# Attention values turned by DMA instead of TensorE, and weight splitting moved to GpSimd, in a fused two-layer transformer kernel

## The chip, the cores and the metric

The kernel runs on one core of a Trainium2 chip. The metric is the device time of one execution in microseconds (us), as the median of several runs. One execution computes all 16 sequences.

## What is computed

The input is `x`, 16 sequences of 256 tokens with 512 features, with a condition vector per sequence. Two blocks follow each other. Cut to what matters:

```python
# block 0
h = layernorm(x) * (1 + scale) + shift
q = h @ Wq.T                      # 16 heads of 32
c = h @ Wkd.T; k = c @ Wku.T; v = c @ Wvu.T   # 4 key/value heads
q, k = rope(q), rope(k)
y = softmax(masked(q @ k.T / sqrt(32))) @ v   # window of 64, block-causal, every 64th key
x = x + y @ Wo.T
# block 1
h = rms(x) * gain1
q, k, v = h @ Wq1.T, h @ Wk1.T, h @ Wv1.T     # 8 heads of 64, one key/value head
x = x + softmax(rope(q) @ rope(k).T / 8) @ v @ Wo1.T
h = rms(x) * gain2
x = x + (silu(h @ Wg.T) * (h @ Wu.T)) @ Wd.T  # inner width 2048
```

"Weighted values", or heads, are `y`: the attention output of all heads of a tile of 128 tokens, a 128x512 matrix, just before the product with `Wo` or `Wo1`.

## The kernel before, in words

**Arithmetic.** Every fp32 operand of a product is split into a high and a low fp16 half, and `product` (L1384 to L1386) issues three matmuls: high by high, high by low, low by high. A product wants its left operand with the features on the partitions, so activations that lie with tokens on the partitions are turned first. Splitting costs one ScalarE copy (the high half) and one VectorE subtraction (the low half).

**Rounds.** Sequences are worked in 8 pairs. A round does both attention blocks of a pair, and among their steps, piece by piece, the MLP of the pair before. The MLP has 96 parts (`mlp_part`, L1594) of 6 matmuls each: 64 for the gate and up products (four parts for each of 16 chunks) and 32 for the down product. `PLAN` (L124) says by hand how many parts go with each named step; `between(m, step)` issues them ahead of that step's own work, on TensorE (L1643) and the matching gate, tanh and sum operations on VectorE and ScalarE. The first round has no MLP to mix in, and after the eighth round the last MLP runs alone.

**Attention.** Each block is a row of units, 24 in block 0 and 16 in block 1. Unit j goes through: scores on TensorE (L1448 or L1454) into one of four PSUM banks; minimum on VectorE; exponentials on ScalarE (L853); high half on ScalarE (L862) and low half on VectorE (L1083) into one of three slots of `prob`; a DMA transpose issued by SyncE (L574, `turn_probs`); values on TensorE into `ybank`. Scores run two units ahead, values four behind. The four banks and the three slots are handed out in a fixed order (`ORDER`, and the unit's number modulo 3), and each use waits until the use before it in the same place is over.

**Heads.** When the values of a tile (s, t) of sequence s and token tile t are complete, `normalise` (VectorE, L1123) writes them to `work`. Then TensorE turns them with four fp32 transposes into the next PSUM bank (`heads`, L1415, shown as L1419), ScalarE takes the high half (`heads`, L839, shown as L842), VectorE the low half (`heads_low`, L1057, shown as L1061), and `project` (L1519) multiplies by `Wo`. For t = 0 this happens inside the unit loop at the units of `FILL_AT` (20 and 22 in block 0, 12 and 14 in block 1); for t = 1 in `finish` (L1504), which is the end of each block: last values, `out{layer}a` projections of t = 0, heads of t = 1, `out{layer}b` projections of t = 1. After these come residual add (L1141), squares on ScalarE (L996), the root on GpSimd (L691), scaling (L1260) and the transposes of the next stage, `fill`.

**Weights.** In the first round weights are loaded by SyncE as fp32 into staging areas and split: most in 128x512 pieces by ScalarE and VectorE (`PIECES_AT`, L151: eight pieces for `wq1` and `wo1`, shown as L1003 and L1335), the four 1 MB groups `wd0` to `wd3` by GpSimd (`big_split_`, L754; per group four operations each at L758, L761 and L766). `SPLIT_AT`, `LOADS_AT` and `RAW_AT` (L156 to L174) name the step at which GpSimd splits, and SyncE loads, a group or one of the first two raw chunks of the gate and up weights. In the second round GpSimd splits these chunks (L734 to L751) as they are first used.

SyncE issues every DMA, in the order of `PLAN`, from one queue.

Of the kernel before, what the change touches and what calls it, by code (L numbers as in the profile page):

```python
# [14 lines left out]
P = 128  # L15
# [46 lines left out]
FILL_AT = [{20: 0, 22: 1}, {12: 0, 14: 1}]  # L62


def unit_uses(layer):
    uses = [(f"unit{layer}", j) for j in range(AHEAD)]
    for j in range(UNITS[layer]):
        if j + AHEAD < UNITS[layer]:
            uses.append((f"unit{layer}", j + AHEAD))
        if j in FILL_AT[layer]:  # L70
            uses.append((f"heads{layer}", FILL_AT[layer][j], 0))
    return uses
# [5 lines left out]
         + unit_uses(0) + [("out0", s, 0) for s in BOTH] + [("heads0", s, 1) for s in BOTH]  # L78
         + [("out0", s, 1) for s in BOTH]
         + [("fill2", s, b) for s in BOTH for b in range(2)] + [("kv1", s) for s in BOTH]  # L80
         + unit_uses(1) + [("out1", s, 0) for s in BOTH] + [("heads1", s, 1) for s in BOTH]
         + [("out1", s, 1) for s in BOTH] + [("fill4", s, b) for s in BOTH for b in range(2)])
# [4 lines left out]
HI_ORDER = ([("fill0", s, b) for s in BOTH for b in range(2)]  # L87
            + [name for layer in range(2) for name in (
                [use for j in range(UNITS[layer]) for use in (
                    [(f"unit{layer}", j)] + [(f"heads{layer}", FILL_AT[layer][k], 0)  # L90
                                             for k in FILL_AT[layer] if k == j])]
                + [(f"heads{layer}", s, 1) for s in BOTH]
                + [(f"fill{2 + 2 * layer}", s, b) for s in BOTH for b in range(2)])])
HI_USE = {name: m for m, name in enumerate(HI_ORDER)}
HI_USES = len(HI_ORDER)
LOW_ORDER = [name for name in HI_ORDER if name[0][:4] != "unit"]
# [8 lines left out]
def last_read(name):  # L105

    kind, k = name[0], name[1]
    if kind[:4] == "unit":
        return "prob_split", sum(UNITS), unit_index(int(kind[4]), k) + 1
# [4 lines left out]
    if kind in ("kv", "kv1"):  # L114
# [9 lines left out]
PLAN = [("fill0.0", 0), ("fill0.1", 3), ("lat.0", 3), ("lat.1", 2), ("kv.0", 2), ("kv.1", 1),  # L124
# [1619 lines left out]
```

## Time and profile before

| | before |
|---|---|
| median of 3 runs | 1868.71 us (1867.02 to 1870.58) |
| the profiled execution's own time | 1865.45 us |
| its span | 1863.6 us |
| TensorE (PE) busy | 1730.3 us, 93% |
| VectorE (DVE) busy | 1148.2 us, 62% |
| ScalarE (ACT) busy | 941.9 us, 51% |
| GpSimd (POOL) busy | 375.1 us, 20% |
| DMA queue of SyncE, share of 16 engines | 57.1% |

The rounds follow from where the transposes of `fill4` (L1411) stand: the first round ends at about 214 us, the second at 442 us, the following six take 211 to 218 us each, and the last MLP runs from 1736 us on. Reported times of neighbouring matmuls overlap, because their ends are modelled; what a matmul costs is the distance from its start to the next one's start. PEclk is the granted TensorE clock, 1.00 being 2.4 GHz and 0.50 being 1.2 GHz.

### The profile page before, as it was taken

What the parts mean: (1) busy time and instruction counts of PE and PEld (TensorE: products, weight loads), DVE (VectorE), ACT (ScalarE), POOL (GpSimd) and SP (SyncE); (2) the same over time, 40 slices, a digit from 0 to 9 for tenths busy, and PEclk for the clock granted to TensorE, in tenths of its full rate; (3) what the DMA queues carried; (4) which work ended last, traced back from release to release, by engine and by line L of the source; (5) the groups of instructions that cost most, each with busy time, mean ns of one, the idle gap of its engine ahead of it and who ended that gap; (6) DMA issues with size and microseconds to landing.
All of it is one profiled execution on the core that took longest, in us unless ns stands there. A gap on an engine that the chain in (4) does not pass through costs nothing.

```text
span 1863.6 us, 38242 instructions
## 1 busy us (share of the span) xinstructions
PE 1730.3 (93%) x12496; PEld 956.0 (51%) x12496; DVE 1148.2 (62%) x2960; ACT 941.9 (51%) x2783; POOL 375.1 (20%) x530
## 2 busy tenths in 40 slices
PE   6675998999999999999999999999999999999999
PEld 5543544455455544555455654555445554555444
DVE  5668567575676647675576746776476745757320
ACT  3646447354574547554483545645374544826320
POOL 2343377111110111110110111111111111101120
PEclk9577999999999999999999999999999999999999
DMA  5965479461793538663584717844386625936220
GB/s 180 218 157 100 132 178 228 123 121 55 161 181 90 82 99 187 144 107 83 120 184 92 120 68 156 173 97 79 107 190 132 113 74 133 185 89 108 96 69 23
DMA packets 527352, 234.51 MB, mean 126 GB/s; under 512 B 476432, under 2 KB 493840, under 8 KB 527120
## 3 DMA queue, kind: packets, MB, share of 16 engines
q1 hardware_dynamic: 527120, 231.72, 57.1%
q8 instruction: 108, 1.77, 0.4%
q14 instruction: 124, 1.02, 0.2%
HBM read 90.09 MB, written 16.78 MB: 57 GB/s over the span
## 4 chain that ended last, share of the span: by engine, by line
PE 70%; DMA 10%; DVE 7%; ACT 5%; issue 4%; SPq 3%; POOL 0%; DVEq 0%; ACTq 0%
PE up L1384 7%; PE gate L1386 7%; PE gate L1384 7%; PE gate L1385 7%; PE up L1385 7%; PE up L1386 7%; DMA prob_t<-prob 7%; PE y L1384 4%; PE y L1386 4%; PE y L1385 4%; PE bank L1384 3%; PE bank L1386 3%; PE bank L1385 3%; PE bank L1411 2%; ACT bank L853 2%
## 5 line engine op out<-in xcount | busy, mean ns | idle before, releaser
L853 ACT ACTIVATE bank<-bank,low 128x128 f32<-128x128 f32 (+2 forms) x768 | 303.9, 397 | 85.2 <-DVE low L1076 71.5
L697 POOL TENSOR_TENSOR inner_t<-inner,inner_t 128x512 f16<-128x512 f32 x128 | 148.5, 1160 | 697.0 <-ACT inner_t L1021 697.0
L1083 DVE TENSOR_TENSOR prob<-bank,prob 128x512 f16<-128x512 f32 (+1 forms) x320 | 203.1, 635 | 71.5 <-ACT prob L862 69.2
L862 ACT ACTIVATE prob<-bank 128x512 f16<-128x512 f32 (+1 forms) x320 | 179.1, 560 | 89.6 <-DMA prob_t<-prob 63.2
L1384 PE MATMUL up<-mlp,ring 128*128 128x512 f16 x512 | 195.3, 381 | 10.6 <-DVE inner L1351 10.6
L1341 DVE SCALAR_TENSOR_TENSOR silu<-silu,gate 128x512 f32<-128x512 f32 x128 | 87.9, 687 | 181.6 <-ACT silu L1015 181.6
L1384 PE MATMUL gate<-mlp,ring 128*128 128x512 f16 x512 | 195.0, 381 | 0.8 <-POOL ring L751 0.7
L1386 PE MATMUL gate<-mlp,ring 128*128 128x512 f16 x512 | 195.5, 382 | 0.0
L1385 PE MATMUL gate<-mlp,ring 128*128 128x512 f16 x512 | 195.4, 382 | 0.0
L1385 PE MATMUL up<-mlp,ring 128*128 128x512 f16 x512 | 194.9, 381 | 0.0
L1386 PE MATMUL up<-mlp,ring 128*128 128x512 f16 x512 | 194.7, 380 | 0.0
L853 ACT ACTIVATION_READ_ACCUMULATOR bank<-bank,low 128x1 f32 x768 | 159.8, 208 | 0.0
L1072 DVE CUSTOM_DVE_ANT_0 bank<-bank,mask 128x193 f32<-128x193 f32 (+1 forms) x512 | 152.3, 351 | 5.8 <-PE bank L1448 5.8
L1015 ACT ACTIVATE silu<-gate 128x512 f32<-128x512 f32 x128 | 76.0, 594 | 136.1 <-PE gate L1386 129.6
L1351 DVE SCALAR_TENSOR_TENSOR inner<-up,silu 128x512 f32<-128x512 f32 x128 | 88.1, 688 | 85.5 <-PE up L1386 78.2
L996 ACT ACTIVATE work<-x_mid 128x512 f32<-128x512 f32 x64 | 40.3, 630 | 177.0 <-DVE x_mid L1141 177.0
L1384 PE MATMUL y<-v_hi,prob_t 128*128 128x32 f16 (+2 forms) x1024 | 110.6, 186 | 18.3 <-DMA prob_t<-prob 13.0
L1021 ACT ACTIVATE inner_t<-inner 128x512 f16<-128x512 f32 x128 | 81.2, 634 | 77.9 <-DVE inner L1351 77.9
L1385 PE MATMUL y<-v_lo,prob_t 128*128 128x32 f16 (+2 forms) x1024 | 109.2, 185 | 0.0
L1386 PE MATMUL y<-v_hi,prob_t 128*128 128x32 f16 (+2 forms) x1024 | 109.1, 185 | 0.0
L1076 DVE TENSOR_REDUCE low<-bank 128x2 f32<-128x512 f32 x128 | 86.9, 684 | 32.8 <-PE bank L1454 32.7
L1384 PEld LDWEIGHTS y<-v_hi,prob_t 128*128 128x128 f16 (+1 forms) x1024 | 91.4, 99 | 29.6 <-DMA prob_t<-prob 19.2
(166 smaller groups left out, 4039.0 us busy)
## 6 DMA issues: line engine op xcount, KB each, us to landing
ring<-wgu_dram SPq DMA_DIRECT2D x112, 512.0 KB, 3.7
x_in<-x_dram SPq DMA_DIRECT2D x18, 512.0 KB, 5.8
x_res<-x_mid SPq DMA_DIRECT2D x16, 512.0 KB, 3.0
wgu_dram<-ring SPq DMA_DIRECT2D x16, 512.0 KB, 3.6
out_dram<-x_res SPq DMA_DIRECT2D x32, 256.0 KB, 3.0
prob_t<-prob SPq DMA_TRANSPOSE x256, 3.3
inner_t<-wd_t_dram SPq DMA_DIRECT2D x8, 512.0 KB, 4.7
ring<-wg_t_dram SPq DMA_DIRECT2D x16, 256.0 KB, 3.8
```

Of the source, the lines that this page charges most:

```text
L697: pool.tensor_tensor(inner_t[:, 1, f, :], inner[:], inner_t[:, 0, f, :], ALU.subtract).then_inc(inner_low, 1)
L853: ins = act.activation(bank_[:, at:at + wid], bank_[:, at:at + wid], ACT.Exp, bias=low[:, j % BANKS, k:k + 1], scale=-1.0, accum_out=total)
L862: act.activation(terms(prob[:, g % SLOTS, 0, :], layer, j), terms(work_bank[USE[f"unit{layer}", j] % BANKS][:], layer, j), ACT.Copy).then_ ...
L1021: act.activation(inner_t[:, 0, f, :], inner[:], ACT.Copy).then_inc(inner_high, 1)
L1072: ins = dve.tensor_tensor_reduce(out=view, in0=view, in1=mask[:, 0:wid], scale=1.0, scalar=3.0e38, op0=ALU.add, op1=ALU.min, accum_out=low ...
L1076: ins = dve.tensor_reduce(low[:, j % BANKS, 0:2], bank_[:].rearrange("p (h k) -> p h k", h=2), AX.X, ALU.min)
L1083: dve.tensor_tensor(terms(prob[:, slot, 1, :], layer, j), terms(work_bank[USE[name] % BANKS][:], layer, j), terms(prob[:, slot, 0, :], lay ...
L1341: dve.scalar_tensor_tensor(silu[:], silu[:], 1.0, gbank[:], ALU.add, ALU.mult).then_inc(gated, 1)
L1351: dve.scalar_tensor_tensor(inner[:], ubank[:], 0.5 * HS / (WS * WS), silu[:], ALU.mult, ALU.mult).then_inc(inner_ready, 1)
L1384: pe.matmul(out_ap, left[0], right[0], start=start, stop=False)
L1385: pe.matmul(out_ap, left[0], right[1], start=False, stop=False)
L1386: return pe.matmul(out_ap, left[1], right[0], start=False, stop=stop)
```

## The change

The TensorE transposes of the heads are gone. ScalarE now takes the high half of `work` in token order into a slot of `prob`, VectorE the low half beside it, and SyncE issues one DMA transpose of both halves (eight blocks of 128x128 fp16) into the operand `act` of the projection. The heads no longer take one of the four PSUM banks, but do take one of the three `prob` slots, so that units and heads together are numbered (`SPLIT`). In block 0 the heads of t = 0 move from units 20 and 22 to 13 and 15.

`wq1` and `wo1` are split by GpSimd, at the start of the first round, in place of ScalarE and VectorE. Loads and splits of the `wd` groups and of the first two raw chunks move from the units of block 0 to its end and beyond. `PLAN` is dealt out anew. The diff, cut to its core (of `PLAN` the end of block 0 and of block 1 are shown whole; among the rest, units 12 to 16 of block 0 go from 1, 1, 1, 1, 2 parts to 2, 3, 1, 2, 0, and `query3.1`, `stack2.0`, `scores1`, units 2, 5 and 11 of block 1 lose one part each):

```diff
-FILL_AT = [{20: 0, 22: 1}, {12: 0, 14: 1}]
+HEADS_AT = [{13: 0, 15: 1}, {12: 0, 14: 1}]
...
-        if j in FILL_AT[layer]:
-            uses.append((f"heads{layer}", FILL_AT[layer][j], 0))
...
+SPLIT_ORDER = split_order(0) + split_order(1)
+SPLIT = {name: m for m, name in enumerate(SPLIT_ORDER)}
+SPLITS = len(SPLIT_ORDER)
...
-        ("out0a.0", 0), ("out0a.1", 0), ("heads0.0", 1), ("heads0.1", 0), ("out0b.0", 0),
-        ("out0b.1", 0), ("fill2.0", 2), ("fill2.1", 1), ("kv1.0", 1), ("kv1.1", 0),
+        ("out0a.0", 0), ("out0a.1", 0), ("heads0.0", 1), ("heads0.1", 0), ("out0b.0", 2),
+        ("out0b.1", 0), ("fill2.0", 2), ("fill2.1", 0), ("kv1.0", 1), ("kv1.1", 0),
...
-        ("unit1_14", 1), ("unit1_15", 0), ("out1a.0", 0), ("out1a.1", 0), ("heads1.0", 2),
-        ("heads1.1", 0), ("out1b.0", 1), ("out1b.1", 0), ("fill4.0", 2), ("fill4.1", 1)]
+        ("unit1_14", 1), ("unit1_15", 0), ("out1a.0", 0), ("out1a.1", 1), ("heads1.0", 3),
+        ("heads1.1", 1), ("out1b.0", 0), ("out1b.1", 0), ("fill4.0", 1), ("fill4.1", 1)]
...
-             "unit0_1": range(10, 11),
-             "out0a.0": range(11, 13), "out0a.1": range(13, 15), "unit1_1": range(15, 16),
-             "unit1_3": range(16, 17), "unit1_5": range(17, 18), "unit1_7": range(18, 19)}
-BIG = [f"wd{c}" for c in range(CH)]
-SPLIT_AT = {"fill2.0": BIG}
+             "unit0_1": range(10, 11)}
+BIG = ["wq1", "wo1"] + [f"wd{c}" for c in range(CH)]
+SPLIT_AT = {"fill0.0": BIG[:2], "heads0.0": BIG[2:3], "kv1.0": BIG[3:5], "unit1_6": BIG[5:]}
...
-LOADS_AT = {"keys.1": [("wkv1", 0), ("wkv1", 1)], "unit0_1": [("wd0", 0)],
-            "unit0_2": [("wd0", 1)], "unit0_4": [("wd1", 0)], "unit0_5": [("wd1", 1)],
-            "unit0_7": [("wq1", 0)], "unit0_8": [("wq1", 1)], "unit0_10": [("wd2", 0)],
-            "unit0_11": [("wd2", 1)], "unit0_14": [("wd3", 0)], "unit0_15": [("wd3", 1)],
-            "fill2.0": [("wo1", 0), ("wo1", 1)]}
-RAW_AT = {"unit0_18": 0, "unit0_20": 1}
+LOADS_AT = {"lat.0": ["wkv1"], "kv.0": ["wo1"], "out0a.0": ["wd0"], "out0a.1": ["wd1"],
+            "heads0.0": ["wd2"], "heads0.1": ["wd3"]}
+RAW_AT = {"fill2.0": 0, "kv1.0": 1}
...
-            for key in ("tw1", "tw2", "wo0"):
+            for key in ("wo0", "tw1", "tw2", "wq1"):
...
+            def turn_heads(n, layer, s, t):
+                split = SPLIT[f"heads{layer}", s, t]
+                need_apart(sp, prob_split, count(n, SPLITS, split + 1), (cond_used, 1))
+                sp.dma_start(act_both[s][:, :, :, t * P:(t + 1) * P].rearrange(
+                    "p a c q -> p (a c) q"), prob[:, split % SLOTS].rearrange("p a k -> p (a k)"),
+                             transpose=True).then_inc(heads_in[s], 16)
...
             def heads(n, layer, s, t):
-                use = USE[f"heads{layer}", s, t]
-                need(act, full, count(n, USES, use + 1))
-                act.activation(act_t[s][0][:, :, t * P:(t + 1) * P],
-                               work_bank[use % BANKS][:].rearrange("p (c q) -> p c q", c=CH),
+                name = (f"heads{layer}", s, t)
+                need(act, weighted, count(n, 8, 4 * layer + 2 * t + s + 1))
+                turned_before(act, n, name)
+                act.activation(prob[:, SPLIT[name] % SLOTS, 0, :], work[:, s, t, :],
                                ACT.Copy).then_inc(hi_done, 1)
...
             def heads_low(n, layer, s, t):
...
-                dve.tensor_tensor(act_t[s][1][:, :, cols],
-                                  work_bank[use % BANKS][:].rearrange("p (c q) -> p c q", c=CH),
-                                  act_t[s][0][:, :, cols], ALU.subtract).then_inc(low_made, 1)
+                dve.tensor_tensor(prob[:, slot, 1, :], work[:, s, t, :], prob[:, slot, 0, :],
+                                  ALU.subtract).then_inc(prob_split, 1)
...
-            def heads(n, layer, s, t):
-                bank_ = bank_for(n, f"heads{layer}", s, t)
-                need(pe, weighted, count(n, 8, 4 * layer + 2 * t + s + 1))
-                for c in range(CH):
-                    ins = pe.transpose(bank_[:, c * P:(c + 1) * P],
-                                       work[:, s, t, c * P:(c + 1) * P], ident[:])
-                ins.then_inc(full, 1)
...
             def project(n, layer, s, t, w):
                 bank_ = bank_for(n, f"out{layer}", s, t)
-                need(pe, low_made, count(n, LOW_USES, LOW_USE[f"heads{layer}", s, t] + 1))
+                need(pe, heads_in[s], heads_count(n, layer, t))
                 token_major(bank_[:], act_t[s], t, w, D).then_inc(full, 1)
```

## Rows read from the trace of the kernel before

Columns of a busy-time row: the stretch, its length, busy us and instructions of PE, PEld (weight loads), DVE, ACT and POOL, then PEclk, DMA share, GB/s. Columns of a timeline row: start, us, engine, line, operation, what it writes and reads, how many.

**Rows 1.** Busy time by stretch: first round, a middle round, the last MLP alone.
```profile
0.00:214.00 214.00, 143.96 (x1127) 101.36 (x1128) 141.02 (x380) 114.02 (x341) 73.61 (x120) 0.77 0.69 162
...
869.00:1087.00 218.00, 210.11 (x1546) 114.48 (x1546) 139.24 (x364) 115.74 (x345) 30.75 (x45) 0.99 0.58 121
...
1736.00:1864.00 128.00, 124.36 (x577) 56.15 (x574) 25.54 (x37) 21.34 (x35) 18.50 (x16) 1.00 0.20 68
```

**Rows 2.** Waits, 442 to 1736 us (six rounds): us in total, times, longest.
```profile
ACT prob L862 <- DMA prob_t<-prob: 38.1, 39, 2.7
...
PE bank L1448 <- DVE prob L1083: 7.0, 12, 1.2
...
PE bank L1384 <- DVE act_lo L1061: 4.8, 6, 1.0
...
PE bank L1419 <- DVE prob L1083: 3.5, 3, 1.5
```

**Rows 3.** TensorE's timeline around eight of the heads' transposes.
```profile
1070.96 1.04 PE L1419 MATMUL bank<-ident,work 128*128 128x128 f32 x8
1071.84 0.38 PE L1384 MATMUL up<-wd_hi,inner_t 128*128 128x512 f16 x1
```

**Rows 4.** Timeline at the end of block 0 and of block 1, a middle round.
```profile
990.88 0.38 PE L1384 MATMUL gate<-mlp,ring 128*128 128x512 f16 x1
...
991.46 0.24 DVE L1127 RECIPROCAL inv<-sums 128x16 f32<-128x16 f32 x1
...
1068.37 0.38 PE L1384 MATMUL up<-wd_hi,inner_t 128*128 128x512 f16 x1
...
1069.09 0.69 DVE L1129 TENSOR_TENSOR work<-y,inv 128x512 f32<-128x512 f32 x1
```

**Rows 5.** Line L574, the DMA transposes of `prob`: durations of the issue, time to landing.
```profile
L574 SPq DMA_TRANSPOSE prob_t<-prob x256: 1231/1237/3755, 61.2 to 1710.5; - x128
...
DMA to landing us min/median/max: 3.0/3.3/6.4
```

**Rows 6.** Busy time by stretch at the ends of the two blocks.
```profile
990.00:994.00 4.00, 2.90 (x37) 1.89 (x33) 2.91 (x6) 1.81 (x4) 0.00 (x0) 1.00 0.00 0
1068.00:1072.00 4.00, 3.99 (x33) 2.53 (x34) 1.71 (x5) 1.12 (x3) 0.00 (x0) 1.00 0.00 0
```

**Rows 7.** SyncE's timeline in the first round, units of block 0.
```profile
82.44 2.09 SPq L574 DMA_TRANSPOSE x_mid<-prob  x1
...
110.16 4.11 SPq L574 DMA_TRANSPOSE prob_t<-prob  x3
```

**Rows 8.** DMA issues by line, 84 to 110 us: KB, us to landing.
```profile
prob_t<-prob SPq DMA_TRANSPOSE x9, 4.8
```

**Rows 9.** DMA queues and issues, 154 to 196 us, units of block 1.
```profile
q1 hardware_dynamic: 16896, 4.20, 58.6%
...
prob_t<-prob SPq DMA_TRANSPOSE x12, 3.2
```

**Rows 10.** Busy time by stretch, two pieces of the first round.
```profile
8.00:10.00 2.00, 1.07 (x6) 1.10 (x6) 0.00 (x0) 0.00 (x0) 1.75 (x4) 1.00 1.04 403
32.00:34.00 2.00, 1.63 (x10) 1.29 (x11) 0.77 (x4) 0.13 (x1) 0.00 (x0) 0.50 0.00 0
```

**Rows 11.** The chain that ended last, first round, end of block 0.
```profile
119.12 0.70 DVE work L1129
...
121.25 0.70 DVE act_lo L1061
...
122.09 0.38 PE bank L1384
```

**Rows 12.** Groups by line: VectorE's pieces of the `wo` weights.
```profile
L1335 DVE SCALAR_TENSOR_TENSOR wo_lo<-inner_t,wo_hi 128x512 f16<-128x512 f32 x8 | 5.3, 694 | 3.9 <-ACT wo_hi L1003 3.9
```

**Rows 13.** Line L766, GpSimd's low halves of `wd`: ns min, median, max.
```profile
L766 POOL TENSOR_TENSOR wd_lo<-inner_t,wd_hi x16: 1150/1152/1154, 77.0 to 111.5; 128x512 f16<-128x512 f32 x16
```

**Rows 14.** Line L1171, VectorE's sums of two fp32 operands in SBUF.
```profile
L1171 DVE TENSOR_TENSOR work<-work x96: 281/681/1639, 39.6 to 1671.6; 128x512 f32<-128x512 f32 x64, 128x256 f32<-128x256 f32 x16, 128x128 f32<-128x128 f32 x16
```

More of the change, by code:

```diff
@@ L256, in build @@
         work = sb("work", [P, PAIR, TILES, D])
-        act_t = [halves(f"act{s}", [P, CH, TOK]) for s in BOTH]
+        act_both = [sb(f"act{s}", [P, 2, CH, TOK], F16) for s in BOTH]
+        act_t = [(a[:, 0], a[:, 1]) for a in act_both]
         mlp = sb("mlp", [P, 2, CH, PTOK], F16)
@@ L397, in build @@
                "wkv1": (0, [(wide(wk1_t), CH, HD1, 0), (wide(wv1_t), CH, HD1, CH * HD1)]),
-               "wq1": (0, by_two(wq1_t)), "wo1": (0, by_two(wo1_t))}
-        for k, key in enumerate(BIG):
-            at = int(key[-1])
-            raw[key] = ((3, 1, 2, 3)[k], by_two(wd_t[at * D:(at + 1) * D, :]))
+               "wq1": (3, [(wide(wq1_t), CH, D, 0)]), "wo1": (1, [(wide(wo1_t), CH, D, 0)])}
+        for c, slot in enumerate((2, 3, 1, 0)):
+            raw[f"wd{c}"] = (slot, [(wide(wd_t[c * D:(c + 1) * D, :]), CH, D, 0)])
         landed, older, got = {}, {}, (STAGES + 2) * [0]
@@ L409, in build @@
             (key, w, p * PIECE, p * PIECE, PIECE) for key, w, pieces in (
-                ("wq0", wq0, 4), ("wo0", wo0, 4), ("wkv1", None, 1), ("wq1", wq1, 4),
-                ("wo1", wo1, 4)) for p in range(pieces)]
+                ("wq0", wq0, 4), ("wo0", wo0, 4), ("wkv1", None, 1)) for p in range(pieces)]
         def staged(key):
@@ L437, in big_views @@
         def big_views(key, half):
-            slot, at = staged(key), int(key[-1])
-            return [(slot[:, c * D:(c + 1) * D],
-                     flat(wd[half])[:, (at * CH + c) * D:(at * CH + c + 1) * D])
+            slot = staged(key)
+            w, at = ((wq1, 0) if key == "wq1" else (wo1, 0) if key == "wo1" else
+                     (wd, int(key[-1]) * CH))
+            return [(slot[:, c * D:(c + 1) * D], flat(w[half])[:, (at + c) * D:(at + c + 1) * D])
                     for c in range(CH)]
@@ L480, in _, with load @@
         def _(sp):
-            def load(key, which=None):
+            def load(key):
                 slot, parts = raw[key]
@@ L484, in load @@
                     split_wait(sp, k)
-                for src, chunks, cols, at in parts if which is None else [parts[which]]:
+                for src, chunks, cols, at in parts:
                     dst = staged(key)[:, at:at + chunks * cols]
@@ L569, in turn_probs @@
                 g = unit_index(layer, j)
-                need_apart(sp, prob_split, count(n, sum(UNITS), g + 1), (cond_used, 1))
+                split = SPLIT[f"unit{layer}", j]
+                need_apart(sp, prob_split, count(n, SPLITS, split + 1), (cond_used, 1))
                 need_apart(sp, pv_done, count(n, sum(UNITS), g - TURNED + 1), (cond_used, 1))
@@ L647, in _ @@
                 turn((None, 0), step)
-                for key, which in LOADS_AT.get(step, ()):
-                    load(key, which)
+                for key in LOADS_AT.get(step, ()):
+                    load(key)
                 if step in RAW_AT:
@@ L1080, in prob_lows @@
             def prob_lows(n, layer, j):
[L1081 removed]
+                name = (f"unit{layer}", j)
+                slot = SPLIT[name] % SLOTS
                 need(dve, hi_done, count(n, HI_USES, HI_USE[name] + 1))
```

83 lines of the change are left out of this document (46 added, 37 removed), and 20 rows, old and new, of the table PLAN.

## The prediction, made before the changed kernel was run

> **What bounds the kernel now.** I read busy time by stretch first [rows 1]. In a middle round TensorE is busy 210 of 218 us, so whatever leaves its queue is gained there, as long as no wait takes its place. The first round is another matter: 144 of 214 us, a mean clock of 0.77 and DMA engines at 0.69; it is set by chains of waits. The last MLP, 96 parts in 128 us, gives the price of one part, 1.33 us; I take 1.3. It isn't touched. Next come the waits of the six middle rounds [rows 2]: TensorE waits little, but four kinds of wait there belong to what the change moves. Last I read the timeline at the ends of the blocks, since that is where the heads of t = 1 stand between the last values and the next projection with nothing but MLP parts to cover them [rows 4].
>
> **Middle rounds: what is removed.** Eight transposes take the distance from 1070.96 to 1071.84, 0.88 us [rows 3]. A round has 8 heads of 4, that is 32, so 3.5 us of TensorE's queue go.
>
> Three waits go too [rows 2], each divided by six rounds. The projection's wait for `act_lo`, 4.8 us, is 0.8 per round. The transposes' wait for a PSUM bank (DVE prob L1083), 3.5 us, is 0.6. The scores' wait for a bank, 7.0 us, is 1.2; where heads take a bank, the scores behind them get one that was released a unit later, and without heads this shift is gone. Not all of it stems from there, so I take 0.7 (bounds 0 and 1.2). Together 2.1.
>
> **Middle rounds: what is added.** The heads of t = 0 are asked for several units after they are ready and cost TensorE nothing; that rests on SyncE and the slots keeping pace (a rival below). For t = 1 the new path is: both normalisations, the high half on ScalarE beside the second of them, the low half, SyncE's issue, the transpose, the projection. What is queued behind the projection's wait is all of TensorE's work. Behind SyncE's wait for the low half are only loads and stores with rounds of slack; the issue itself holds SyncE 1.24 us [rows 5], eight times a round.
>
> In block 0 the second reciprocal starts at 991.46 and lasts 0.24; with 0.69 for the normalisation it ends at 992.42 [rows 4]. A low half of 0.70 [rows 11] and 0.1 for SyncE (estimate) give 993.2. From issue to landing takes 3.0 at best, 3.3 in the median and 6.4 at worst [rows 5]. I take 3.3, because in exactly these stretches the DMA engines are idle, share 0.00 [rows 6]; so 996.5. TensorE is through with the values at 990.88 and has three parts, 3.9 us, until 994.8. New wait: 1.7 us (1.4 at the best landing, 4.8 at the worst).
>
> In block 1 the second normalisation ends at 1069.78; the same steps give 1073.9. TensorE has four parts from 1068.37 on, until 1073.6. New wait: 0.3 (0 to 3.4). The second sequence's heads are issued 1.24 later and are covered by the first projection, which is as long as two parts (24 issues; 2.6 us).
>
> The parts dealt out anew uncover other places: `fill2.1` and `fill4.0` lose one part each, just where the scaled residual is awaited. One part is 1.3, so the bounds are 0 and 2.6 together; I take 0.6. Block 1 starts its units three parts earlier, with VectorE idle until then, but sends two more uses through three slots; 0.4, bounds -1 and 3.
>
> Sum for a round: -3.5 - 2.1 + 1.7 + 0.3 + 0.6 + 0.4 = **-2.6**. Seven rounds carry an MLP: **-18.2**. The second round has more on the DMA engines, but gets the same.
>
> **First round.** Its MLP-free chain gains and loses.
>
> Units of block 0. SyncE turns unit 9 at 82.44, and units 21 to 23 from 110.16 to 114.27, the last from about 113 on [rows 7]: 2.2 us a unit. In this stretch a transpose lands after 4.8 us [rows 8]; in block 1, without loads between, after 3.2 [rows 9]. There the queue was used for 58.6% of 42 us by 16 transposes: 1.54 us each, a limit even without loads. Once the loads are moved away I expect 1.65 a slot, but the two heads (units 13 and 15) take slots too: 16 x 1.65 = 26.4 in place of 14 x 2.2 = 30.6, so -4.2 (bounds -8 and 0, the latter if ScalarE sets the pace).
>
> End of block 0. From the end of the first normalisation, 119.82, to the projection at 122.09 took 2.3 us [rows 11]. Now: second normalisation 0.93, low half 0.70, 0.1, landing 3.3, together 5.0: +2.7. Two groups `wd0` and `wd1` are loaded ahead of it; at 403 GB/s [rows 10] a megabyte takes 2.7 us, so they are through about when the heads are issued. `wd2` stands in SyncE's queue between the two heads: the second lands 1.24 + 0.6 + 2.7 = 4.5 after the first, of which the first projection covers 2.6: +1.9. Together +4.6 (bounds 2.5 and 10). End of block 1: +2.7, with nothing loaded there.
>
> Splitting of `wq1` and `wo1`. Eight pieces of 0.69 leave VectorE [rows 12] and eight copies ScalarE. The four of `wq1` lay beside a projection and give nothing; the four of `wo1` lay in the units of block 1. 4 x 0.69 = 2.8 at most; I take -1.5.
>
> GpSimd instead. Its low halves last 1.15 each [rows 13]. VectorE's sums of two operands that both lie in SBUF have a median of 0.68 but a longest of 1.64 [rows 14]: they are held up by up to 1 us. Before, GpSimd split the `wd` groups during the units of block 0, where VectorE reads PSUM. Now it splits `wq1` and `wo1` during the first queries and keys, and `wd1` and `wd2` during those of block 1, where such sums and subtractions stand on the chain, some 12 in each place. At 0.2 us each that is +5 (bounds 0 and 15). The Trainium skill has a rule for this (SBUF — State Buffer, SBUF: two separate sides): VectorE and GpSimd share a port pair under an exclusive lock that is held for a whole instruction, and VectorE needs it when it has two SBUF inputs while GpSimd reads SBUF. The spread in that row agrees with it.
>
> Clock. The clock was at 0.50 in 32:34, after TensorE had been short of work [rows 10]. The two new waits of 5 us may bring the same, with projections at half speed for a while: +1.5 (0 to 5).
>
> Sum: -4.2 + 4.6 + 2.7 - 1.5 + 5 + 1.5 = **+8.1**.
>
> **Forecast.** -18.2 + 8.1 = -10.1. The profiled execution took 1865.45, so 1855.4; the median of the runs lies 3.3 above it, so **1858.6** as a median.
>
> **Rivals.**
>
> Much more gained. All four waits go entirely (-2.6), and the new ones are covered by parts as dealt: -5.2 a round with 0.9 of new waits, -36 in seven rounds, first round even: 1833. For it: the DMA engines are idle at the places that matter, and VectorE is idle before block 1's units. Against it: the sum above leaves block 0 uncovered by 1.7.
>
> Slower, at the ends of the blocks. The place is the projection of t = 1, 14 times in seven rounds. If the transpose lands after 4.8, as under load, and not 3.3, each costs 1.5 more: +21, so 1880. It decides from 10.1 / 14 = 0.7 more on, a landing of 4.0. Against it: share 0.00 [rows 6]; for it: the destination is cut into more places than before, and `act` was never written by a DMA. The Trainium skill speaks against the change itself (VectorE: DVE Perf Modes, Rules for kernel authors): a 128x128 transpose belongs on TensorE if PSUM will do as destination, and on the DMA only otherwise. Read by duration that would make this rival the likely one; the rows above make it depend on cover.
>
> Slots. ScalarE already waits for a slot 38.1 us in six rounds [rows 2], and none of it reaches TensorE. Four more uses at 1.5 us are 6 us a round. Should half of this reach TensorE: +21, again 1880.
>
> First round worse. Splits and subtractions hold each other up at their bound, +10 more, 1869; or GpSimd comes late to the root: 1874.
>
> The change doesn't do what it says. If the round is really paced by ScalarE and VectorE and TensorE merely looks full, the 3.5 us turn into waits: about +8 in all, 1877. TensorE's few waits speak against it.
>
> **How the numbers follow.** The forecast with its neighbours (1850 to 1867) gets 0.42, much more gained 0.20, the end of the blocks 0.14, the slots 0.05, the first round 0.12, no effect 0.07. A measurement of this kernel can tell about 0.2%, 3.7 us. Faster by more than that, below 1865.0: the forecast nearly whole, and the second case, 0.62. Within it: part of the first-round case and the edge of the forecast, 0.13. Slower, above 1872.4: 0.25. The range leaves out a tenth at either end: 1838 to 1878.
>
> **What would show it.** Right: no L1419 in the profile; TensorE's waits for the DMA into `act` near 1.7 us at the end of block 0 and under 1 at the end of block 1; middle rounds of 213 to 214 us by the distance of their `fill4` transposes; a first round of about 222 us, with the units of block 0 shorter by 4 us and VectorE's L1171 and L1238 longer there. Wrong: a landing above 4 us in the middle rounds, waits of ScalarE for slots that TensorE's scores inherit, or a first round that is not longer.

## The result: slower, and outside the range

The median of the changed kernel is 1883.43 us (1879.21 to 1885.25, four runs) against 1869.3 of the kernel before (1867.02 to 1870.58): ratio 1.007, 95% interval 1.0051 to 1.0089. Forecast were 1858.6 us and a range of 1838 to 1878.

The page of the kernel after. A group of section 5 reads: line, engine, operation, tiles, count | busy us, mean ns of one | idle just before them and what ended most of it.

```profile
PE 1712.4 (91%) x12240; PEld 924.2 (49%) x12240; DVE 1150.1 (61%) x2952; ACT 941.8 (50%) x2775; POOL 401.8 (21%) x554
...
q1 hardware_dynamic: 594608, 248.51, 61.0%
...
L1405 PE MATMUL bank<-wo_hi,act 128*128 128x512 f16 x256 | 100.7, 393 | 35.8 <-DMA act<-prob 35.3
...
L1461 PE MATMUL bank<-k_t,q_t 96*128 96x193 f16 (+1 forms) x512 | 71.8, 245 | 42.9 <-DVE prob L1104 30.1
```

The heads' transposes are gone, and before the projection (L1405) TensorE now sits idle for 35.3 us until the DMA into `act` has landed; only the scores (L1461) have a longer idle time. L1405 is the line of the first product (before: L1384), L1461 the scores, L883 and L1104 ScalarE's and VectorE's split of the probabilities, L863 and L1082 that of the heads.

The waits of the six middle rounds, 450 to 1750 us of the kernel after (us, times, longest), beside [rows 2]:

```profile
PE bank L1405 <- DMA act<-prob: 18.7, 21, 1.9
PE bank L1461 <- DVE prob L1104: 13.4, 16, 1.4
PE bank L1432 <- issue: 7.9, 5, 1.8
...
PE gate L1405 <- DVE silu L1362: 5.2, 6, 1.1
PE y L1405 <- DMA prob_t<-prob: 4.7, 11, 0.9
...
PE y L1405 <- DMA x_mid<-prob: 2.7, 3, 1.2
...
ACT prob L883 <- DMA prob_t<-prob: 70.8, 59, 2.5
...
ACT prob L883 <- DMA x_mid<-prob: 31.6, 18, 3.5
```

ScalarE's waits for a slot of `prob` went from 38.1 (46.6 with those ended by the turns into `x_mid`) to 102.4. The scores' wait rose from 7.0 to 13.4. The heads' own path, as bounded in [rows 5], is on the page of its line:

```profile
L592 SPq DMA_TRANSPOSE act<-prob x64: 1231/1246/1990, 89.9 to 1735.3; - x64
...
DMA to landing us min/median/max: 3.1/3.2/6.5
```

Where the time lies is best seen by rounds: the distance from the first transpose of `stack` by TensorE to the first of the next round. "First" goes from the start of the span to the second round's mark, "middle" is the mean of five rounds, "rest" goes from the last such mark to the end of the span. These are us of one profiled execution; the last column is the median of the runs.

| kernel | heads | slots | first | second | middle | rest | median |
|---|---|---|---|---|---|---|---|
| before | TensorE | 3 | 207.8 | 229.6 | 216.1 | 345.5 | 1869.3 |
| after | DMA | 3 | 218.0 | 224.9 | 218.4 | 342.6 | 1883.4 |
| plan_only | TensorE | 3 | 207.4 | 224.8 | 215.5 | 342.4 | 1849.3 |
| weights_only | TensorE | 3 | 202.5 | 229.1 | 217.8 | 345.0 | 1868.1 |
| plan_and_weights | TensorE | 3 | 203.1 | 223.5 | 215.1 | 341.6 | 1845.4 |
| heads_and_plan | DMA | 3 | 224.4 | 226.8 | 218.9 | 343.7 | 1894.1 |
| tensor_slots4 | TensorE | 4 | 199.8 | 220.4 | 212.4 | 339.2 | 1824.8 |
| slots4 | DMA | 4 | 217.1 | 222.9 | 215.3 | 338.8 | 1860.2 |
| t0_by_dma | t=0 DMA | 3 | 211.8 | 228.0 | 216.8 | 343.6 | 1870.3 |
| t1_by_dma | t=1 DMA | 3 | 212.9 | 225.8 | 215.5 | 343.1 | 1862.8 |

So the first round grew by 10.2 us from before to after, the middle rounds by 2.3 each; the second round and the rest became shorter by 4.7 and 2.9.

### The profile page after: what moved, and what is told of

It reads as the page before. It is cut to its first block, busy times and chain, and to the rows that moved or that the text cites. A ratio compares the mean times of both kernels' runs of the same rounds, so it can differ in the third digit from the quotient of the medians.

```text
span 1877.4 us, 37983 instructions
## 1 busy us (share of the span) xinstructions
PE 1712.4 (91%) x12240; PEld 924.2 (49%) x12240; DVE 1150.1 (61%) x2952; ACT 941.8 (50%) x2775; POOL 401.8 (21%) x554
## 4 chain that ended last, share of the span: by engine, by line
PE 55%; DMA 16%; DVE 11%; issue 7%; ACT 6%; SPq 4%; DVEq 0%; POOL 0%; ACTq 0%
DMA prob_t<-prob 8%; PE gate L1405 5%; PE gate L1407 5%; PE gate L1406 5%; PE up L1405 5%; PE up L1406 5%; PE up L1407 5%; DMA act<-prob 5%; PE bank L1405 4%; PE bank L1407 3%; PE bank L1406 3%; PE y L1405 3%; PE y L1407 3%; PE y L1406 3%; SPq L585 3%
## 5 line engine op out<-in xcount | busy, mean ns | idle before, releaser
L1104 DVE TENSOR_TENSOR prob<-bank,prob 128x512 f16<-128x512 f32 (+1 forms) x320 | 203.2, 635 | 104.3 <-ACT prob L883 103.3
L883 ACT ACTIVATE prob<-bank 128x512 f16<-128x512 f32 (+1 forms) x320 | 178.4, 558 | 143.7 <-DMA prob_t<-prob 91.3
L1405 PE MATMUL gate<-mlp,ring 128*128 128x512 f16 x512 | 195.1, 381 | 6.1 <-DVE silu L1362 5.2
L1405 PE MATMUL up<-mlp,ring 128*128 128x512 f16 x512 | 195.8, 382 | 5.3 <-DVE inner L1372 5.3
L1372 DVE SCALAR_TENSOR_TENSOR inner<-up,silu 128x512 f32<-128x512 f32 x128 | 88.0, 688 | 86.8 <-PE up L1407 79.0
L1405 PE MATMUL bank<-wo_hi,act 128*128 128x512 f16 x256 | 100.7, 393 | 35.8 <-DMA act<-prob 35.3
L1405 PE MATMUL y<-v_hi,prob_t 128*128 128x32 f16 (+2 forms) x1024 | 110.3, 186 | 15.3 <-DMA prob_t<-prob 13.2
L1461 PE MATMUL bank<-k_t,q_t 96*128 96x193 f16 (+1 forms) x512 | 71.8, 245 | 42.9 <-DVE prob L1104 30.1
```

Source lines behind the costliest of these rows:

```text
L883: act.activation(terms(prob[:, SPLIT[name] % SLOTS, 0, :], layer, j), terms(work_bank[USE[f"unit{layer}", j] % BANKS][:], layer, j), ACT.C ...
L1104: dve.tensor_tensor(terms(prob[:, slot, 1, :], layer, j), terms(work_bank[USE[name] % BANKS][:], layer, j), terms(prob[:, slot, 0, :], lay ...
L1372: dve.scalar_tensor_tensor(inner[:], ubank[:], 0.5 * HS / (WS * WS), silu[:], ALU.mult, ALU.mult).then_inc(inner_ready, 1)
L1405: pe.matmul(out_ap, left[0], right[0], start=start, stop=False)
```

## The experiments

**Which part of the change did it.** Four kernels hold the new heads (H), the new table of parts `PLAN` (P) and the new splitting and loading of the weights (W) in different mixtures. weights_only is before with W, plan_only before with P, heads_only before with H, heads_and_plan after without W.

```diff
 # weights_only: of the change only this, with the loads that go with it
-SPLIT_AT = {"fill2.0": BIG}
+SPLIT_AT = {"fill0.0": BIG[:2], "heads0.0": BIG[2:3], "kv1.0": BIG[3:5], "unit1_6": BIG[5:]}
 # plan_only: of the change only the numbers of PLAN, as
-("unit1_2", 1), ("unit1_5", 2), ("unit1_11", 1), ("unit1_12", 1)
+("unit1_2", 0), ("unit1_5", 1), ("unit1_11", 0), ("unit1_12", 2)
```

> The kernel before with the weights part of the change alone: wq1 and wo1 split by GpSimd, wd and raw chunks loaded later; heads stay on TensorE, PLAN as before. Theory (shared SBUF port): the first round grows by 5 to 8 us because VectorE's two-operand sums during the first queries and keys are held up; median 1874 to 1877; the sum L1171/L1192 reaches 1.5 us or more before 60 us. Rival (the first round's extra 10 us come from the heads): no change, 1869 within 2. The middle rounds stay at 216 us under both.

> Only PLAN dealt out as in the change; heads on TensorE, weights as before. Theory: fewer parts in block 1 leave its units to ScalarE's pace, so middle rounds grow by 0 to 3 us, median 1869 to 1890. Rival (the new PLAN is better in itself, and the loss is all in the DMA path): below 1869.

> The changed kernel with the weights part undone (wq1, wo1 by ScalarE and VectorE, wd split early). Theory: the first round falls by 5 to 8 us against the changed kernel, middle rounds keep their 218 us; median 1875 to 1878. Rival: as slow as the changed kernel, 1883.

> Only the heads turned by DMA; weights and PLAN as before. At the end of block 0 one part covers the new path instead of three, at the end of block 1 two instead of four: theory (uncovered path) says 2.6 us more of waiting in each, less what the parts give elsewhere; middle rounds of 219 to 222 us, median 1885 to 1900. Rival (slots of prob set the pace, cover does not matter): like heads_and_plan, within 4 us of it.

Measured: weights_only 1868.12, ratio 0.9996 (0.9974 to 1.0019); plan_only 1849.25, 0.9902 (0.9865 to 0.994); heads_and_plan 1894.08, 1.0146 (1.0108 to 1.0184); heads_only 1979.46, 1.0609 (1.0568 to 1.065). Of the four theories only the sign of the heads' cost held. weights_only took the time of its rival (no change), plan_only fell where its rival had it (below 1869), heads_and_plan lies above both of its cases, and heads_only is 79 us above the top of its theory. The table of parts, which I had taken for a detail, brings about 1%; the heads cost more than all else. heads_only shows how tightly the two are bound: with the old table the projections wait 9.3 us a round for `act` (3.1 in after), and the middle rounds last 230 us.

**The best without the heads.** plan_and_weights is after with the heads on TensorE again.

```diff
-                need(pe, heads_in[s], heads_count(n, layer, t))
+                need(pe, low_made, count(n, LOW_USES, LOW_USE[f"heads{layer}", s, t] + 1))
 # and heads(...) with its four pe.transpose of work into a bank, at the old places,
 # in block 0 units 20 and 22; so H below is the DMA together with the move to units 13 and 15
```

> The kernel after with the heads (weighted values) turned on TensorE as before: the new plan and the new splitting of the first round's weights stay. If the change's three parts add, the turn of the heads by DMA alone costs what separates this kernel from the kernel after: plan alone gave 0.990 of before, and the weights part took 5.3 us off the first round when it stood alone and 6.4 us off it beside DMA heads. Expected: first round ended at 202 +- 2 us, and 1838 to 1846 us in all, 0.983 to 0.988 of before. The rival, from weights_only, where the whole time stayed the same though the first round was 5.3 us shorter: what the weights part gains in the first round is given back later, and this kernel stands at 1847 to 1852 us.

Measured: 1845.44 (1840.98 to 1846.22), ratio 0.9873 (0.9846 to 0.99), the first round 203.1. So in the final mixture P gives -18 (against before in its own series, 1867.5), W -4 and H +38, together +16 where the result shows +14. W is the weak one of the three: -4 here, -11 beside DMA heads, 0 alone, and only its gain in the first round (4 to 6 us) shows in all three pairs of profiles.

The waits of plan_and_weights, 450 to 1740 us:

```profile
PE bank L1439 <- DVE prob L1074: 9.2, 7, 1.6
...
PE bank L1402 <- issue: 2.2, 5, 0.6
...
PE y L1375 <- DMA prob_t<-prob: 0.9, 2, 0.6
```

These are the scores, the fill's transposes and the values: 1.5, 0.4 and 0.2 us a round, against 2.2, 1.3 and 0.8 in after; and in after 3.1 us for `act`, 0.9 for `silu` and 0.5 for `x_mid` come on top. Only 1.3 us a round of waits for banks and low halves before the heads' transposes and the projections go. The busy time by stretch (450 to 1740) says the same in one number, TensorE's idle time:

```profile
450.00:1740.00 1290.00, 1257.20 (x9252) 682.33 (x9250) 826.22 (x2160) 693.45 (x2054) 187.67 (x269) 0.99 0.59 124
```
```profile
450.00:1740.00 1290.00, 1222.50 (x8993) 652.34 (x8992) 824.33 (x2163) 685.43 (x2046) 182.36 (x263) 1.00 0.63 132
```

The first fence is plan_and_weights, 32.8 us idle in 6.00 rounds; the second is the kernel after, 67.5 in 5.91. That is 5.5 and 11.4 us a round: 5.9 us of new idle time for 3.5 us of transposes. By the table the round is 3.3 us longer.

**Slots, or the tiles?** The rise of ScalarE's waits pointed to the slots. slots4 is after with a fourth one, laid on the latent buffers; t0_by_dma and t1_by_dma are after with only one tile's heads by DMA. In t1_by_dma the first tile's heads, back on TensorE, stay in block 0 at units 13 and 15, where after turns them by DMA; in plan_and_weights they stand at 20 and 22. So its distance from plan_and_weights holds this move too.

```diff
 # slots4
-        SLOTS, TURNED = 3, LAG + 1
-        prob = sb("prob", [P, SLOTS, 2, 512], F16)
+        SLOTS, TURNED = 4, LAG + 1
+        prob = sb("prob", [P, SLOTS - 1, 2, 512], F16)   # the fourth slot lies in lat_all
 # t0_by_dma (t1_by_dma: (1,)); the other tile's heads on TensorE, HEADS_AT as in after
+DMA_T = (0,)
```

> The kernel after with four slots for the split probabilities and values in place of three (the fourth lies on the latent buffers, which are free while the units run). Theory 'slots': heads share the three slots with the units, each slot is held until SyncE's turn has landed (3 to 6.5 us), and ScalarE waits for slots 102 us over the middle rounds against 47 before; then most of the 2.2 us of a middle round that separate the kernel after from plan_only come back, the middle round falls from 218.4 to 216.5 or less, the first round from 218.0 to under 212, and the kernel takes 1850 to 1866 us. Rival 'latency at the block ends': the wait is for the turn of the last heads itself, with nothing left to do beside it, and a fourth slot doesn't shorten that: ScalarE's waits for slots fall under 50 us and the time stays within 1876 to 1886 us.

> The kernel after with only the heads of the first tile of a block (t=0, which come due while units still run) by DMA; those of the second tile (t=1, at the end of the block) on TensorE again, 16 transposes of them in place of 32. Theory 'block ends': the exposed part is the second tile's turn, about 3 us in a middle round and 10 us in the first; without it 1850 to 1862 us, faster than before, first round ended at 204 to 210. Theory 'slots and SyncE's queue': half of the cost stays, 1862 to 1874 us.

> The reverse: only the heads of the second tile by DMA, those of the first tile on TensorE. Theory 'block ends': all of the cost stays and the gain of 16 transposes goes: 1880 to 1890 us, first round ended at 216 to 222. Theory 'slots and SyncE's queue': half the uses of slots go, and it comes to 1862 to 1874 us.

Measured: slots4 1860.22 (ratio 0.9952, 0.9934 to 0.997), t0_by_dma 1870.31 (1.0017, 1.0 to 1.0034), t1_by_dma 1862.8 (0.9971, 0.9955 to 0.9986). The number for slots4 is the one that the theory of the slots gave, and ScalarE's waits for slots in it fell from 102 to 23 us. t1_by_dma, for which the theory of the block ends wanted 1880 or more, fell where the slots wanted it. On these three alone I would have called the slots the cause. The control says otherwise:

```diff
 # tensor_slots4: the same edit of the slots in plan_and_weights
-                             prob[:, g % SLOTS].rearrange("p a k -> p (a k)"),
+                             prob_slots[g % SLOTS].rearrange("p a k -> p (a k)"),
```

> The control for the fourth slot: plan_and_weights (heads on TensorE, new plan, new splitting) with four slots for the probabilities in place of three. ScalarE waits 47 us for slots over the middle rounds there. Theory 'three slots are short only because of the heads': the fourth slot gives at most 0.5 us a round here against 3.3 us a round with the heads in the slots, so 1841 to 1846 us, and heads by DMA with four slots (1860.2 us) remain 14 to 19 us slower than heads on TensorE. Rival 'three slots are short in either kernel': 1825 to 1838 us.

Measured: 1824.82 (1823.26 to 1825.7), ratio 0.9769 (0.9745 to 0.9792). The rival holds. The fourth slot is worth 21 us with heads on TensorE and 23 with heads by DMA; the heads cost 38 us with three slots and 35 with four. Slots are short in either kernel; they are at most a small part of why the heads by DMA are dear. tensor_slots4 also beats both kernels of this case.

The waits of tensor_slots4, and then of slots4, 450 to 1740 us:

```profile
PE bank L1443 <- DVE prob L1078: 4.4, 6, 1.0
...
PE bank L1406 <- issue: 2.7, 5, 0.6
```
```profile
PE bank L1409 <- DMA act<-prob: 19.1, 18, 2.1
PE bank L1436 <- issue: 7.8, 5, 1.9
...
PE y L1409 <- DMA x_mid<-prob: 4.8, 6, 1.3
...
PE y L1409 <- DMA prob_t<-prob: 3.1, 8, 1.0
...
PE y L1409 <- DMA x_mid<-lat_all: 1.1, 3, 0.5
```

With slots in plenty the wait for `act` alone is 19.1 us in six rounds, 3.2 a round: nearly the 3.5 us that the transposes cost.

**The two tiles with four slots, and the place.** t0_slots4 and t1_slots4 join both edits. t0_late has three slots and moves the first tile's heads of block 0.

```diff
 # t0_late, on t0_by_dma
-HEADS_AT = [{13: 0, 15: 1}, {12: 0, 14: 1}]
+HEADS_AT = [{17: 0, 19: 1}, {12: 0, 14: 1}]
```

> t0_by_dma with four slots: only the first tile's heads by DMA. With three slots they cost 24.9 us against heads on TensorE (1870.3 against 1845.4). Theory 'the first tile hurts by holding slots': with four they cost at most 8 us, 1825 to 1833 us, and nearly all of slots4's 35 us is the second tile's bare latency. Rival 'SyncE's order and latency hurt, not the slots': 1840 to 1852 us.

> t1_by_dma with four slots: only the second tile's heads by DMA. With three they cost 17.4 us (1862.8 against 1845.4). Theory 'bare latency at the ends of the blocks, whatever the slots': 15 to 28 us more than tensor_slots4, 1840 to 1853 us, with the first round 9 us or more longer than its 199.8. Rival: under 1835 us, and the cost of both together in slots4 isn't the sum of the two.

> t0_by_dma (three slots) with the first tile's heads of block 0 split and turned at its units 17 and 19 in place of 13 and 15; there are 24 units and the heads are needed after the last. Theory 'place': at 13 and 15 the split and the turn are queued on ScalarE and SyncE before units that TensorE wants next; later units have the same problem, so the time changes by less than 4 us from 1870.3, unless the values are only just ready at unit 13, when it falls to 1856 to 1866. Rival 'too late': at 19 the turn comes close to the first projection and the time rises to 1874 or more.

Measured: t0_slots4 1844.41 (0.9859, 0.9839 to 0.9878); t1_slots4 1858.68 (0.9945, 0.9926 to 0.9963); t0_late 1883.11 (1.0081, 1.0062 to 1.01). By medians:

| heads by DMA | none | t = 0 | t = 1 | both |
|---|---|---|---|---|
| 3 slots | 1845.4 | 1870.3 | 1862.8 | 1883.4 |
| 4 slots | 1824.8 | 1844.4 | 1858.7 | 1860.2 |

The first tile's heads, costed at nothing in the prediction, cost 25 us with three slots and 20 with four, so "SyncE's order and latency, not the slots" (the rival of t0_slots4) stands. The kernels with t = 1 alone are 17 and 34 us above those with none, the latter more than bare latency at the ends was to give. With four slots both together cost hardly more than t = 1 alone: the costs don't add.

Part of this column is not the DMA's. The t = 0 transposes, moved to units 13 and 15 on TensorE, wait there for a PSUM bank, six times in six rounds (t1_by_dma, 450 to 1740 us; t1_slots4 has the same 10.3):

```profile
PE bank L1470 <- DVE prob L1132: 10.3, 6, 1.8
```

That is 1.7 us a round. plan_and_weights, with them at 20 and 22, has 0.3 in this place, tensor_slots4 none. No run has all heads on TensorE at units 13 and 15, so what the move costs by itself isn't measured, in these two kernels or in H.

t0_late came out as its rival "too late" had it in time, but not in cause: the wait for `act` stayed near that of t0_by_dma (9.3 us), and a new one appeared.

```profile
PE gate L1433 <- DVE silu L1390: 27.1, 6, 4.9
PE bank L1433 <- DMA act<-prob: 8.4, 12, 1.2
```

Six times in six rounds, 4.5 us each, TensorE waits for the MLP's `silu`. The timeline of one of them shows where the delay starts:

```profile
769.35 0.50 ACT L903 ACTIVATE prob<-bank 128x386 f16<-128x386 f32 x1 [4.19 <-DMA prob_t<-prob]
770.37 0.69 DVE L1390 SCALAR_TENSOR_TENSOR silu<-silu,gate 128x512 f32<-128x512 f32 x1 [4.48 <-ACT silu L1056]
```

ScalarE stands 4.2 us before a unit's split, until a slot of `prob` is free; the tanh behind it in ScalarE's queue comes late, then VectorE's product, then TensorE. All six waits look like this, and so do five of the six, 0.8 to 1.1 us long, that after has for `silu`; in the kernels with four slots there are none. So a lack of slots does reach TensorE by this way. Four units' delay of two splits is +13 us.

**Can parts cover the end of block 0?** slots4_cover is slots4 with two parts taken from the units and put at the end of the block.

```diff
-("unit0_12", 2), ("unit0_13", 3), ... ("heads0.0", 1), ("heads0.1", 0)
+("unit0_12", 1), ("unit0_13", 2), ... ("heads0.0", 2), ("heads0.1", 1)
```

> slots4 with two of the parts laid against the end of block 0: one from the 12th and one from the 13th unit of block 0 go to the wait for the second tile's heads (2 x 1.34 us of TensorE work). Theory 'the wait of the block's end is bare time': with work beside it the act<-prob waits of the middle rounds (19.1 us over six of them in slots4) fall by 1 to 2 us a round and the units can spare the parts: 1847 to 1856 us. Rival 'the parts cover the units just as much': they fall as far and the waits for probabilities rise as far, 1857 to 1864 us.

Measured: 1880.87, ratio 1.0077 (1.0054 to 1.01), worse than both theories. Its waits, 450 to 1740 us:

```profile
PE y L1409 <- DMA prob_t<-prob: 24.4, 22, 2.7
PE bank L1409 <- DMA act<-prob: 15.8, 18, 1.6
```

The wait for `act` fell by 3.3 us and that for the probabilities of the units rose by 21.3 (3.1 before). The parts weren't spare in the units: they hid the turns of the units' probabilities.

**What a long wait costs.** warm lets TensorE repeat the first tile's projection into the bank it is going to overwrite, while it waits, at the end of both blocks. It was meant for the first round alone, but `n[0]` is None in the second round too, so that 48 matmuls more run there as well, among an MLP that leaves TensorE little idle time.

```diff
                 bank_ = bank_for(n, f"out{layer}", s, t)
+                if n[0] is None and (s, t) == (0, 1):
+                    for _ in range(2):
+                        token_major(bank_[:], act_t[s], 0, w, D)
                 need(pe, heads_in[s], heads_count(n, layer, t))
```

> The kernel after, with 24 matmuls thrown away (a repeat of the first tile's projection into the bank that the real one then overwrites) while TensorE waits for the second tile's heads, in the first round alone, at the end of both blocks. In the kernel after that wait is 5.67 us at the end of block 1, and the 24 projections behind it take 8.3 us in place of the 5.35 us that they take where TensorE came to them busy; the granted clock is 0.50 from 205 to 210 us. Theory 'the wait costs twice, as itself and as half a clock behind it': the projections behind it are back at 5.4 us, and the first round ends 2 to 5 us sooner than 218.0, at 213 to 216. Rival 'the projections are slow for their own reasons (the data landing late)': the first round ends at 218 or later. The whole time: 1878 to 1882 us by the first, 1883 to 1886 by the second.

After, end of block 1 in the first round: TensorE's timeline and the busy time by stretch (the two numbers before the last are the granted clock and the DMA share).

```profile
205.35 0.59 PE L1405 MATMUL bank<-wo_hi,act 128*128 128x512 f16 x1 [5.67 <-DMA act<-prob]
205.74 0.63 PE L1406 MATMUL bank<-wo_lo,act 128*128 128x512 f16 x1
...
213.25 0.38 PE L1407 MATMUL bank<-wo_hi,act 128*128 128x512 f16 x1
```
```profile
200.00:205.00 5.00, 0.00 (x0) 0.00 (x0) 2.64 (x5) 1.73 (x4) 0.00 (x0) 0.95 0.36 70
205.00:210.00 5.00, 4.65 (x11) 1.60 (x12) 0.00 (x0) 0.00 (x0) 0.00 (x0) 0.50 0.19 35
```

The same place in warm:

```profile
207.08 0.39 PE L1405 MATMUL bank<-wo_hi,act 128*128 128x512 f16 x1 [0.41 <-DMA act<-prob]
...
212.05 0.38 PE L1407 MATMUL bank<-wo_hi,act 128*128 128x512 f16 x1
```
```profile
205.00:210.00 5.00, 4.58 (x22) 1.97 (x21) 0.12 (x1) 0.00 (x0) 0.00 (x0) 1.00 0.55 105
```

In after the first projection behind the wait runs with a granted clock of 0.50, the lower of the two levels (1.2 GHz), 0.43 us from one matmul to the next in place of 0.22. The 24 matmuls take 8.3 us; in warm, with the clock at 1.00 (2.4 GHz), they take 5.35. So the wait of 5.67 us cost another 2.9 behind it. The projections confirm the clock.

The first round ended at 216.8, 1.2 us sooner, less than the expected 2 to 5. But warm is already 2 us behind after when its first thrown-away matmul starts, at 118.0 us: so much two profiles of the same program differ. At the end of block 0 nothing is gained; from the transposes of `fill2` behind it to the end of the round warm takes 83.0 us in place of 86.8, 3.8 less. The whole time was 1884.15 (1.0082, 1.0058 to 1.0106), no gain against after; it says nothing on the clock, since the second round, with its 48 matmuls, took 237.4 us in place of 224.9.

## Why the prediction was wrong, point by point

**The ends of the blocks in the middle rounds: nearly right in mechanism and size.** For the end of block 0 I had worked out a new wait of 1.7 us. In after it reads:

```profile
1006.99 0.39 PE L1405 MATMUL bank<-wo_hi,act 128*128 128x512 f16 x1 [1.79 <-DMA act<-prob]
```

Landing took the 3.2 us in the median that I had taken (3.3), so the rival of a late landing, 4.8, did not happen, though its 1880, which is the slots' time too, was the closest of all. Together the waits for `act` are 3.1 a round in place of 2.0; at the end of block 1 0.2 to 0.8 us is lost in three places, the first tile's projections among them.

**The step that failed in the middle rounds: "the heads of t = 0 ... cost TensorE nothing".** That rested on need and readiness at TensorE. t0_by_dma puts 24.9 us on them, t0_slots4 19.6. TensorE's waits in t0_by_dma, 450 to 1740 us:

```profile
PE y L1433 <- DMA prob_t<-prob: 13.9, 19, 1.3
PE bank L1499 <- DVE prob L1132: 12.8, 18, 1.0
PE bank L1433 <- DMA act<-prob: 9.3, 12, 1.2
```

The last line contradicts the step directly. In block 1 these heads are turned at units 12 and 14 of 16, and their own projections then wait 0.5 and 1.0 us, 1.6 a round (0.4 with four slots). The other two are waits of the units: 2.3 us a round for the turned probabilities and 2.1 for a bank, in place of 0.2 and 1.5 in plan_and_weights. The heads' split sits in the in-order queues of ScalarE and VectorE among the units' splits, and their turn in SyncE's among the probabilities' turns, 1.24 us each; what comes behind them comes later. The size is measured, for the DMA and the move to units 13 and 15 together; that the queues make it is read from those waits and from t0_late, and was not isolated. I had bounded the slots' rival with half of 6 us a round reaching TensorE and given it 0.05; the delay was real, the reason in that form wrong, since a fourth slot leaves 35 of the 38 us.

**The waits that would go.** I took 2.1 a round off; 1.3 went. The 0.7 of the scores' wait for a bank was a choice between 0 and 1.2, and the scores' wait rose by 0.7 against plan_and_weights. The 0.8 for the projection's wait for `act_lo` was not the heads' to give: in plan_only, with the heads on TensorE, it is gone too. H is worth +3.3 us in a middle round by the table, where the sum had -3.6 without the terms of the plan.

**The first round: the end of block 0 was right, the units of block 0 too, the rest not.** The first sequence's fill after block 0 stands at 131.20 in after and at 126.57 in plan_and_weights: +4.6, as predicted to the tenth. Its parts say that some of this is luck: the first projection of t = 1 starts 3.3 us later (I had 2.7), the second sequence's then waits 0.55 (I had 1.9). Of the units of block 0, SyncE's timeline in after shows the last four turns:

```profile
103.53 5.83 SPq L585 DMA_TRANSPOSE prob_t<-prob  x4
```

They are through at 109.4, where the kernel before ended at 114.3 [rows 7]. From the turn of unit 9 to the last one it is 27.0 us in place of 30.6: -3.6 against -4.2. But that gain belongs to W: in plan_and_weights it is 24.2, and the heads take 2.8 of it back. In the profile of after this doesn't show at the end of the units, because they start 2.8 us sooner than in plan_and_weights; warm, the same program up to there, doesn't have this lead. Block 1 I had given +2.7 at its end. From the same two traces: its units +3.5 (the last split starts 60.8 us after that fill in place of 57.3), and its end to the next fill +6.8. Of the 6.8, 3.8 lie before the projection of t = 1, where I had 2.7, and 2.9 are the half-speed projections, for which the term "clock +1.5" stood: a term for both blocks, less than one of them cost. The heads cost the first round +17 (207.4 to 224.4, plan_only to heads_and_plan) or +15 (203.1 to 218.0); my terms for them there come to +8.8, and to 3.3 more for their two slots in the -4.2. For the units of block 1, where the heads cost 3.5 us, I had nothing.

**GpSimd and VectorE: the term of +5 was right in kind, rather too small.** VectorE's sums with both operands in SBUF, lines up to 214 us, before and after:

```profile
L1171 DVE TENSOR_TENSOR work<-work 128x512 f32<-128x512 f32 (+2 forms) x12 | 6.4, 572 | 0.0
```
```profile
L1192 DVE TENSOR_TENSOR work<-work 128x512 f32<-128x512 f32 (+2 forms) x12 | 10.8, 941 | 0.0
```

Twelve take 4.4 us longer while GpSimd splits weights, six of them (+2.5) beside `wq1` and `wo1` in block 0 and six (+1.9) in block 1. The last low half of the first queries ends at 56.95 in place of 52.09, and the stretch of the six sums of block 1 is 3.4 us longer; 0.2 us for each of some 24 operations was the estimate. Which of the two engines waits differs from run to run: in warm, the same program up to there, the first two sums take 0.82 us each and GpSimd's low halves of `wq1` at most 1.6; in after these sums take 0.42, but one of the low halves 4.3. The Trainium skill's rule of the exclusive lock on the shared port pair (SBUF — State Buffer, SBUF: two separate sides) agrees with these rows. What I missed is the sign of the whole: W saves 4 to 6 us of the first round in all three pairs, where the turns of block 0, without loads between them, are through sooner.

**The plan: priced by what it uncovers, not by what it covers.** I had +0.6 and +0.4 a round for it; plan_only is 18 us faster than before. By the profiled executions, which show 11 of the 18 us, that lies in the second round (-4.8), in five middle rounds (-3.0) and in the rest (-3.2). In a middle round TensorE's waits for `act_lo`, for `y` until it is normalised, and for `inner` fall from 2.9 to 0.4 us, and those for banks rise by 0.9; the terms of +0.6 and +0.4 had looked at two uncovered places alone. Which of the moved parts bring it, no run tells apart.

**The rule I set aside.** The Trainium skill (VectorE: DVE Perf Modes, Rules for kernel authors) would leave a 128x128 transpose whose result may go to PSUM on TensorE. I let the rows make this depend on cover. The runs side with the rule in this kernel in every pair, by 35 us and more. What the waits point to is not the transpose's own time on the DMA but its latency and the queues it passes on its way.

**The sum.** Sorted by part, the terms were: heads -14 (seven times -3.6 and +0.4 for the slots; +4.6, +2.7 and +1.5 in the first round), plan +4 (seven times +0.6), splitting and loads -1 (-4.2, -1.5, +5). Of the -4.2, +3.3 are the heads' slots. Measured: +38, -18, -4. The heads were missed by 52 us; a miss of 22 the other way in the plan hides nearly half of it. By stretch the first round came out near its sum (+10.2 where +8.1 stood), though by terms that were off both ways; the rounds behind it, with the rest, are 3.6 us longer where -18.2 stood.

**Open.** Why the costs of the two tiles nearly add with three slots and not with four, and how much of it the move to units 13 and 15 is; how the 20 us of t = 0 divide between the queues of ScalarE, VectorE and SyncE; and which parts bring the gain of the plan. The clock has a share that I had not priced: behind 225 us the spells below full clock lose 2 us in tensor_slots4, but 9 in slots4 and in after and 10 in plan_and_weights (stretches of 1 us, one minus the granted clock, summed; an upper bound, since TensorE isn't always busy in them). So up to 7 of the heads' 35 us with four slots lie there, and none of the 38 with three.

## What to carry to other kernels

An operation that moves from a full engine to the DMA keeps its place in every in-order queue that feeds it: price those it delays there, not only who waits for its result. Give a suspected shortage a control in which the suspect is absent: the fourth slot looked like the cause until it helped the other kernel as much. Move one thing at a time in a control: the heads' new place came along with the DMA and was never told apart. And price a table of cover by both ends of each part moved: two parts taken from the units took 3.3 us off one wait, put 21.3 on another, and cost 21 us in all.

## What the runs showed that I had not expected

Behind a wait of 5.67 us TensorE's granted clock was at half, and the work there took 2.9 us longer, so that the wait cost half as much again. A fourth slot of `prob`, on memory that was free, is worth 21 us: 1824.8 us, 2.3% under the kernel before, though the scores and the values of plan_and_weights waited only 10.1 us in six rounds for the probabilities; the fewer spells below full clock may be up to 9 of the 21.
